# Four chained layers on one core: the second layer's first operands rounded inside the first layer's drain, and the last MLP map taken by quarters

## The chip, the core and the metric

The kernel runs on one core of one Trainium2 chip. A core has five engines that work side by side and meet only through semaphores: TensorE (PE in the profile, its weight loads PEld), VectorE (DVE), ScalarE (ACT), GpSimd (POOL) and SyncE (SP), which issues the DMAs here. The metric is the device time of the whole program in microseconds (us). The kernel before took 1287.68 us in the median of three runs (1285.73 to 1287.99).

## What is computed

Four layers follow one another on 16 sequences of 128 x 256 values (batch B = 16, D = 256). The change touches the end of layer 0 and the start of layer 1.

```python
# layer 0, its end: the MLP
ln_out = layernorm(x, ln3_s, ln3_b)
mlp_out = gelu(ln_out @ w1 + b1) @ w2 + b2        # 256 -> 1024 -> 256
x = x + mlp_out
# layer 1, its start: x is z1ss, the context is u1ss; columns 0:128 and 128:256 have their own weights
for i in range(2):
    h = einsum('od,bdl->bol', Wqkv[i], z1ss[:, :, s:e])
    h = h + einsum('od,bdl->bol', Winj[i], u1ss[:, :, s:e])
    chunks.append(h)
q, k, v = split(concatenate(chunks, axis=2), 3, axis=1)     # 16 heads of 64
# then per head: softmax((q + r_w_bias) . k * SCALE) . v, a map Wo, the residual, a norm
```

Layers 2 and 3 (a small attention and a second product of maps with a batch norm) end the program; nothing of them is changed but the address of one tensor.

## The kernel before

**Blocks.** `program` runs two blocks one after the other, `layer0` and `layers123`. Each gives every engine its own list of instructions. All engines meet at the end of a block, so no instruction of the second starts before the last of the first.

**Layer 0** takes the batch in eight pairs. It is a software pipeline of `BODIES` = 13 bodies. In a body several pairs are at different steps, and the order of an engine's work is written out by hand in its `body`: `pairs(step, offset)` does a step for the pair that stands at that offset, and leaves it out where there is none. The last bodies are the drain, with ever fewer pairs. In body 11 the last pair (the eighth) is at the transposes of its normalised values (T2) and the four hidden maps f0 to f3, while the pair before is at its two output maps y0 and y1, one per batch. In body 12 the last pair has its y0 and y1 and nothing else is left. The linear maps take turns in two PSUM banks, and a map may start when the one before it in its bank has been read out.

The hidden values `hid` are eight chunks of 128 features. They are made in four quarters of two chunks each: PE's map f (L529), two readings by ACT into `ring_h` and `ring_g` (L719), a polynomial and a product on DVE (L884, L889), tanh on ACT (L727), and the gate on DVE (L896). Each gate adds one to `h_gate`. PE's y0 waits for `h_gate.at(i, 3)`, the fourth quarter, and then takes all eight chunks, and y1 follows (L538). In PSUM the sum over the chunks is built up in place. DVE adds `x_mlp` and writes `xs` (L905). `x_mlp` is made by POOL (L447).

**Layer 1** takes the batch in eight pairs again. It multiplies in a faster float format (fp32r) and keeps the accuracy by splitting each operand into a rounded high part and the rest: `wzh`, `wih` are high parts of the weights for the input and for the context, `wzl`, `wil` the rests, `zuh`, `zul` the same of the two inputs (`xs` and `l1_ub`). A projection is high x high + high x rest + rest x high for both inputs and both column halves: 12 matmuls (L1722 for q and k, L1726 for v). ACT casts to the high parts (L1890, L1898, L1903). DVE subtracts to get the rests of the inputs (L1987, L1992) and of the `wz` weights (L2034), POOL those of the `wi` weights (L1676). A rest is written over the raw weight. The weights are rounded in twelve parts, `qk0`, `v0`, `qk1`, ..., of which the first `AT_ONCE` = 4 are made at the start of the block and the others one by one in the first eight steps of the first pair. PE starts with three projections, q0, k0 and v0b0. ACT rounds q0 and k0 again into `qh` and `kh`, DVE makes `ql` and `kl` (L1977, L1981) and copies v0b0 (L1972), and by that frees the bank; q0 and v0b0 share one. Then come the steps, 16 per pair: scores (L1740), row maxima (L1950), exponentials (L1861), the division (`norm`, POOL, L1664), the transposes (L1752), the product with v (L1768) and, in the gaps, the next projections. The last map's weights `wo` are loaded at the block's start (L1653), rounded on ACT (L1943) and their rest made on POOL (L1701), ahead of the first step.

In the second block SP first adds each event's starting credit (one instruction each, some 25), and only then issues its first DMA.

Of the kernel before, what the change touches and what calls it, by code (L numbers as in the profile page):

```python
# [87 lines left out]
def program(nc, x, ctx_in, ctxT, smask, cmask, cols_in, rows_in, wqkv_in, wao_in, wq_in, wkv_in, wco_in,  # L88
            w1_in, w2_in, wz_in, wi_in, wo_in, wqk2_in, wvpg_in, theta_in, ww_in, out, dbg=None, phases="ABC"):
    with ExitStack() as ctx:  # L90
        def sb(name, shape, c=ctx):
# [15 lines left out]
        raw_place = ExitStack()  # L107
        wz0_raw, wz1_raw, wi0_raw, wi1_raw = (raw_place.enter_context(nc.sbuf_tensor(n, [P, 3 * NQ], F32)) for n in (
            "wz0_raw", "wz1_raw", "wi0_raw", "wi1_raw"))
# [6 lines left out]
        if "A" in phases:  # L116
            layer0(nc, locals())
        raw_place.close()
        wzl0, wzl1, wil0, wil1 = (ctx.enter_context(nc.sbuf_tensor(n, [P, 3 * NQ], F32R)) for n in (
            "wzl0", "wzl1", "wil0", "wil1"))  # L120
# [12 lines left out]
def layer0(nc, v):  # L133
    (psum, xs, ident, mean_w, cols, half_neg, col) = (v[n] for n in (
        "psum", "xs", "ident", "mean_w", "cols", "half_neg", "col"))
    (l1_weights_in, wz0_raw, wz1_raw, wi0_raw, wi1_raw) = (v[n] for n in (
        "l1_weights_in", "wz0_raw", "wz1_raw", "wi0_raw", "wi1_raw"))
# [14 lines left out]
    with ExitStack() as ctx:  # L152
# [13 lines left out]
        rows = sb("rows", [P, ROWS["bvpg"]])  # L166
# [3 lines left out]
        wkv = sb("wkv", [P, 2, 2 * D])  # L170
        wco = sb("wco", [P, 2, D])
# [8 lines left out]
        cT = sb("cT", [P, 2, TOK])  # L180
# [77 lines left out]
        def start(bank):  # L258
# [24 lines left out]
            sem(f"weights_in_{n}") for n in ("cols", "rows", "qkv", "ao", "kv", "q", "co", "1", "2", "mask"))  # L283
        consts_made = sem("consts_made")
# [59 lines left out]

        block = ctx.enter_context(nc.Block())

        @block.sync
        def _(sp):
# [48 lines left out]
            for w, src, c in ((wz0_raw, "wz_in", 0), (wz1_raw, "wz_in", 1), (wi0_raw, "wi_in", 0),  # L397
                              (wi1_raw, "wi_in", 1)):
                sp.dma_start(w[:, :], v[src][c * P:(c + 1) * P, :]).then_inc(l1_weights_in, 16)
            for g in range(3, R0 + 2):  # L400
# [5 lines left out]
            sp.dma_start(v["ub"][:, :, :], v["ctx_in"].rearrange("b p d -> p b d")[:, 0:2, :])\  # L406
                .then_inc(v["first_u_in"], 16)
            sp.wait_ge(l1_weights_in, 64)
            sp.wait_ge(v["first_u_in"], 16)

        @block.gpsimd
        def _(pool):
# [47 lines left out]

            def body(j, g):
# [12 lines left out]
                units(add_mask, 7)  # L474

# [29 lines left out]
        def _(pe):  # L505
# [35 lines left out]

            def linear(i, g, name):
# [29 lines left out]
                elif name[0] == "f":  # L572
# [3 lines left out]
                    features_out(i, name, w1, m * 2 * P, lnT[2], g)  # L576
                else:
# [125 lines left out]
        def _(act):  # L703
# [57 lines left out]

            def body(j, g):
# [18 lines left out]
                pairs(read, -1, "k")  # L781
                pairs(read, -4, "T2")
# [51 lines left out]
        def _(dve):  # L834
# [134 lines left out]

            def body(j, g):  # L970
# [27 lines left out]
                units(invert, -4)  # L998

# [55 lines left out]
class Turns:  # L1055
# [31 lines left out]
    def reads(self, key):  # L1087
# [5 lines left out]
          (("x2", 2, 2, D), ("x2b", 2, 2, D), ("fin", 2, 2, D)))  # L1093


def third_stage(nc, v, ctx, late, joins):
# [7 lines left out]
    prob, pT, x2, x2b, fin = (late[n] for n in ("l2_prob", "l2_pT", "x2", "x2b", "fin"))  # L1104
# [17 lines left out]
    vpg = sb("vpg", [P, 2, 2, 2, D])  # L1122
# [369 lines left out]
def layers123(nc, v):  # L1492
    (sb_, psum, xs, ident, mean_w, half_neg, col) = (v[n] for n in (
        "sb", "psum", "xs", "ident", "mean_w", "half_neg", "col"))
    (wz0_raw, wz1_raw, wi0_raw, wi1_raw, wzl0, wzl1, wil0, wil1) = (v[n] for n in (
        "wz0_raw", "wz1_raw", "wi0_raw", "wi1_raw", "wzl0", "wzl1", "wil0", "wil1"))
# [8 lines left out]
    with ExitStack() as ctx:  # L1505
# [30 lines left out]
        wi = [[sb(f"wih{c}", [P, 3 * NQ], F32R) for c in range(2)], [wil0, wil1]]  # L1536
        wo = [sb("woh", [P, PAIRS, P], F32R), wol]
        zu = [sb(f"zu{p}", [P, 2, 2, NB, P], F32R) for p in ("h", "l")]
# [7 lines left out]
        ub, first_u_in = v["ub"], v["first_u_in"]  # L1546
# [15 lines left out]
        PARTS = ["qk0", "v0", "qk1", "qk2", "v1", "qk3", "qk4", "v2", "qk5", "qk6", "v3", "qk7"]  # L1562
        AT_ONCE = 4
# [593 lines left out]
```

## Time and profile before

| | before |
|---|---|
| median of 3 runs | 1287.68 us |
| profiled execution, its own time | 1287.96 us |
| its span, first to last instruction | 1286.2 us |
| granted TensorE clock, mean (share of full) | 0.985 |
| PE busy | 1210.8 us (94%) |
| DVE busy | 927.3 us (72%) |
| ACT busy | 825.9 us (64%) |
| POOL busy | 548.8 us (43%) |

The span runs from the first instruction to the last; the time of a run holds a little more around it. Busy time is the sum of an engine's instructions. Matmuls overlap one another and their ends are modelled, so PE's busy time says little of its rate. The last instruction of layer 0 ends at 469.87 us, layers 2 and 3 begin near 1200 us.

### The profile page before, as it was taken

The numbers are of one execution on the slowest core, as the hardware profiler recorded it, in microseconds if no ns is written. First come the engines' busy times: TensorE is split into PE (matmuls) and PEld (weight loads), VectorE is DVE, ScalarE is ACT, GpSimd is POOL, SyncE is SP. The second block draws the span as 40 slices with busy tenths as digits, with TensorE's granted clock in tenths as the row PEclk, the third lists the DMA queues.
The fourth block names the chain that finished last, engine by engine and source line by source line (L and its number), as shares of the span: only waits on it lengthen the run. The fifth ranks groups of instructions, "written<-read, shape, count | busy, mean of one in ns | idle before, by whom it ended". The sixth has DMA issues, their size and how long they took to land.

```text
span 1286.2 us, 29854 instructions
## 1 busy us (share of the span) xinstructions
PE 1210.8 (94%) x10914; PEld 995.1 (77%) x10914; DVE 927.3 (72%) x1835; ACT 825.9 (64%) x2523; POOL 548.8 (43%) x535
## 2 busy tenths in 40 slices
PE   4798999999999869999999999999999999999997
PEld 3677787788887658888888888888888888888675
DVE  4779989889887558776666676766766766666664
ACT  4588978978986548655555555565555555565542
POOL 3456656546644126433333333334333333333443
PEclk8899999999999979999999999999999999999999
DMA  3340000000000000000000000000000100000011
GB/s 105 99 197 19 14 22 9 12 12 17 6 22 1 1 25 2 2 10 1 2 10 2 1 10 2 8 3 2 10 2 2 55 1 2 1 2 2 18 42 41
DMA packets 18575, 25.39 MB, mean 20 GB/s; under 512 B 1424, under 2 KB 17040, under 8 KB 17936
## 3 DMA queue, kind: packets, MB, share of 16 engines
q1 hardware_dynamic: 18448, 23.69, 5.6%
q8 instruction: 81, 1.33, 0.4%
q14 instruction: 46, 0.38, 0.1%
HBM read 21.58 MB, written 2.10 MB: 18 GB/s over the span
## 4 chain that ended last, share of the span: by engine, by line
PE 49%; ACT 7%; DVE 5%; issue 2%; ACTq 0%
PE psum L1722 11%; PE psum L1768 8%; PE psum L1752 8%; PE psum L1740 7%; PE psum L1726 5%; ACT prob L1861 4%; PE psum L1777 3%; ACT pT L1870 1%; DVE l_neg_max L1950 1%; PE psum L1258 1%; PE psum L1322 1%; PE psum L1793 1%; ACT aTh L1876 1%; DVE aTl L1966 1%; PE psum L1272 1%
## 5 line engine op out<-in xcount | busy, mean ns | idle before, releaser
L1664 POOL TENSOR_TENSOR prob<-prob,l_z_inv 128x512 f32<-128x512 f32 x256 | 261.0, 1040 | 440.5 <-DVE l_z_inv L1956 440.5
L1861 ACT ACTIVATE prob<-psum,l_neg_max 128x256 f32<-128x256 f32 x512 | 235.6, 472 | 228.0 <-DVE l_neg_max L1950 227.9
L752 ACT ACTIVATE ring_e<-ring_e,neg_max 128x128 f32<-128x128 f32 x512 | 164.2, 406 | 15.1 <-DVE neg_max L921 15.0
L1950 DVE TENSOR_REDUCE l_neg_max<-psum 128x2 f32<-128x512 f32 x256 | 163.8, 681 | 10.8 <-PE psum L1740 10.8
L1752 PEld LDWEIGHTS psum<-ident,prob 128*128 128x128 f32 x1024 | 109.8, 141 | 49.0 <-issue 45.0
L1768 PE MATMUL psum<-pT,vs 128*64 128x256 f32 x1024 | 138.8, 391 | 3.7 <-DVE aTl L1966 3.5
L1752 PE MATMUL psum<-ident,prob 128*128 128x128 f32 x1024 | 139.9, 280 | 0.0
L459 POOL TENSOR_TENSOR ring_e<-ring_e,cross_add 128x512 f32<-128x512 f32 x64 | 85.7, 1356 | 91.4 <-DVE ring_e L916 91.4
L1961 DVE COPY pT<-psum 128x512 f32<-128x512 f32 x128 | 88.0, 688 | 45.5 <-PE psum L1752 45.3
L459 POOL TENSOR_TENSOR ring_e<-ring_e,self_add 128x512 f32<-128x512 f32 x64 | 85.9, 1356 | 64.0 <-DVE ring_e L916 63.3
L1966 DVE TENSOR_TENSOR aTl<-psum,aTh 128x256 fp32r<-128x256 f32 x128 | 54.3, 425 | 74.6 <-ACT aTh L1876 74.6
L760 ACT COPY ring_t<-psum 128x512 f32<-128x512 f32 x128 | 75.2, 588 | 47.6 <-PE psum L603 46.9
L1861 ACT ACTIVATION_READ_ACCUMULATOR prob<-psum,l_neg_max 128x1 f32 x512 | 104.0, 203 | 0.0
L1768 PEld LDWEIGHTS psum<-pT,vs 128*64 128x64 f32 x1024 | 63.6, 136 | 39.6 <-issue 7.3
L603 PE MATMUL psum<-ident,ring_e 128*128 128x128 f32 x512 | 82.2, 285 | 10.0 <-ACT ring_t L760 9.1
L1740 PE MATMUL psum<-kh,qh 64*128 64x256 f32 x512 | 85.8, 329 | 5.2 <-ACT prob L1861 5.2
L603 PEld LDWEIGHTS psum<-ident,ring_e 128*128 128x128 f32 x512 | 62.0, 145 | 34.6 <-issue 14.3
L921 DVE TENSOR_REDUCE neg_max<-ring_e 128x4 f32<-128x512 f32 x128 | 84.8, 673 | 2.3 <-POOL ring_e L459 2.3
L1722 PE MATMUL psum<-zuh,wzh 128*128 128x256 f32 x256 | 74.4, 291 | 4.7 <-POOL wil L1676 4.7
L1870 ACT COPY pT<-psum 128x512 f32<-128x512 f32 x128 | 76.3, 596 | 0.2 <-PE psum L1752 0.2
L1740 PE MATMUL psum<-kl,qh 64*128 64x256 f32 x512 | 72.9, 278 | 0.0
L1722 PE MATMUL psum<-zuh,wih 128*128 128x256 f32 x256 | 72.8, 284 | 0.0
(190 smaller groups left out, 3181.2 us busy)
## 6 DMA issues: line engine op xcount, KB each, us to landing
wz_raw<-wz_in SPq DMA_DIRECT2D x2, 1536.0 KB, 14.3
wi_raw<-wi_in SPq DMA_DIRECT2D x2, 1536.0 KB, 20.1
x_in<-x SPq DMA_DIRECT2D x8, 256.0 KB, 2.8
cT<-ctxT SPq DMA_DIRECT2D x8, 256.0 KB, 2.8
w<-w_in SPq DMA_DIRECT2D x2, 1024.0 KB, 8.5
l_ub<-ctx_in SPq DMA_DIRECT2D x8, 256.0 KB, 2.8
cg<-ctx_in SPq DMA_DIRECT2D x4, 512.0 KB, 4.2
out<-fin SPq DMA_DIRECT2D x8, 256.0 KB, 2.1
```

The source lines that it names most:

```text
L459: pool.tensor_tensor(e, e, add, ALU.add).then_inc(scores_add.sem, 1)
L603: last = nc.tensor.transpose(turn_bank[:, h * P:(h + 1) * P], ring_e[:, n % RE, h * P:(h + 1) * P], ident[:, :])
L752: last = nc.scalar.activation(e, e, ACT.Exp, bias=neg_max[:, n % RE, h:h + 1])
L1664: pool.tensor_tensor(e, e, z_inv[:, t % RE, h, :].unsqueeze(2).broadcast_to([P, 2, D]), ALU.mult)\
L1722: last = mm(o, w[wp][c][:, at:at + P], zu[xp][:, s, c, :, :].rearrange("p b l -> p (b l)"), **flags)
L1740: last = mm(score_bank[h][:, qt * D:(qt + 1) * D], q[qp][rows, pair % 2, qt, b, :], k[kp][rows, pair % 2, :, b, :], start=(qp, kp) == (0, ...
L1752: last = nc.tensor.transpose(turn_bank[h][:, kt * D + qt * P:kt * D + (qt + 1) * P], prob[:, t % RE, h, qt * D + kt * P:qt * D + (kt + 1) ...
L1768: last = mm(pv_bank[h * HD1:(h + 1) * HD1, :], vs[:, pair // 2 % 2, b, kt, at:at + HD1], pT[:, h, kt * D:(kt + 1) * D], start=kt == 0, sto ...
L1861: last = nc.scalar.activation(prob[:, t % RE, h, qt * D:(qt + 1) * D], score_bank[h][:, qt * D:(qt + 1) * D], ACT.Exp, bias=neg_max[:, t % ...
L1870: nc.scalar.copy(pT[:, 0, :], turn_bank[0]).then_inc(copied[0].sem, 1)
L1950: nc.vector.tensor_reduce(neg_max[:, t % RE, h, :], score_bank[h].rearrange("p (t c) -> p t c", t=2), AX.X, ALU.max, negate=True).then_inc ...
L1961: nc.vector.tensor_copy(pT[:, 1, :], turn_bank[1]).then_inc(copied[1].sem, 1)
```

## The change

Two things are changed.

The first is the last pair's output map. `last_outputs` takes it in eight groups of two chunks: batch 0 with quarters 0 and 1, batch 1 with quarters 0 and 1, then quarters 2 and 3 with the batches in turns. Each group waits for its own quarter.

The second is the rounding of what layer 1 needs for q0, k0 and v0b0. It moves from the start of the second block into body 11 of layer 0 (`ROUNDING`): ACT casts the first columns of q, k and v of the four raw weights into `first_hi`, and both inputs of the first pair into `zu[0]`; DVE makes the rests of the `wz` weights and of the inputs, POOL those of the `wi` weights. The new tensors lie over `wqkv`, `wao`, `wq`, `wkv` and `cT`, which nobody reads any more by then. The first context pair `l1_ub` is loaded right behind the raw weights instead of at the end of layer 0. In layer 1 the parts `qk0` and `v0` fall away, `AT_ONCE` is 2, and ACT and DVE handle q0 and k0 between the first part and the second. `vpg` of the third stage gets another address.

```diff
+        with ExitStack() as c:
+            zu = [c.enter_context(nc.sbuf_tensor(f"zu{p}", [P, 2, 2, 2, P], F32R)) for p in ("h", "l")]
+            first_hi = c.enter_context(nc.sbuf_tensor("first_hi", [P, 4, 4, P], F32R))
...
+        ROUNDING = BODIES - 2
+
+        def early(w):
+
+            return (w[:, 0:2 * NQ].rearrange("p (t c) -> p t c", t=2)[:, :, 0:P],
+                    w[:, 2 * NQ:2 * NQ + D].rearrange("p (t c) -> p t c", t=2))
+
+        def early_inputs(s):
+
+            return (ub[:, :, :] if s else xs[:, 0:NB, :]).rearrange("p b (c l) -> p c b l", c=2)
...
+            sp.dma_start(ub[:, :, :], v["ctx_in"].rearrange("b p d -> p b d")[:, 0:2, :]).then_inc(first_u_in, 16)
             for g in range(3, R0 + 2):
                 next_ctx(g - 2)
...
             sp.wait_ge(w_mask, 16)
-            sp.dma_start(v["ub"][:, :, :], v["ctx_in"].rearrange("b p d -> p b d")[:, 0:2, :])\
-                .then_inc(v["first_u_in"], 16)
-            sp.wait_ge(l1_weights_in, 64)
-            sp.wait_ge(v["first_u_in"], 16)
...
+            def early_rests():
+                for n in (2, 3):
+                    for k, (low, raw) in enumerate(zip(early(lows[n]), early(raws[n]))):
+                        pool.wait_ge(early_hi, 4 * k + n + 1)
+                        pool.tensor_tensor(low, raw, first_hi[:, n, 2 * k:2 * k + 2, :].bitcast(F32), ALU.subtract)
...
                 units(add_mask, 7)
+                if g == ROUNDING:
+                    early_rests()
...
+            def last_outputs(i, g):
+
+                for quarter, b in ((0, 0), (1, 0), (0, 1), (1, 1), (2, 0), (2, 1), (3, 0), (3, 1)):
+                    name = f"y{b}"
+                    ps = bank(name, i) if quarter == 0 else lin(name)
+                    pe.wait_ge(*h_gate.at(i, quarter))
+                    for c in (2 * quarter, 2 * quarter + 1):
+                        last = nc.tensor.matmul(ps[:, 0:D], hid[:, c, b * P:(b + 1) * P], w2[:, c, 0:D],
+                                                start=c == 0, stop=c == F0 // P - 1)
+                    if quarter == 3:
+                        filled(name, last, g)
...
+                elif g == R0 - 1:
+                    if name == "y0":
+                        last_outputs(i, g)
...
+            def early_rounding():
+                act.wait_ge(l1_weights_in, 64)
+                act.wait_ge(first_u_in, 16)
+                for k in range(2):
+                    for n, raw in enumerate(raws):
+                        nc.scalar.copy(first_hi[:, n, 2 * k:2 * k + 2, :], early(raw)[k]).then_inc(early_hi, 1)
+                    nc.scalar.copy(zu[0][:, k, :, :, :], early_inputs(k)).then_inc(early_zu_hi, 1)
...
                 pairs(read, -1, "k")
+                if g == ROUNDING:
+                    early_rounding()
                 pairs(read, -4, "T2")
...
+            def early_rests():
+                for k in range(2):
+                    for n in range(2):
+                        dve.wait_ge(early_hi, 4 * k + n + 1)
+                        nc.vector.tensor_tensor(early(lows[n])[k], early(raws[n])[k],
+                                                first_hi[:, n, 2 * k:2 * k + 2, :].bitcast(F32), ALU.subtract)
+                    dve.wait_ge(early_zu_hi, k + 1)
+                    nc.vector.tensor_tensor(zu[1][:, k, :, :, :], early_inputs(k), zu[0][:, k, :, :, :].bitcast(F32),
+                                            ALU.subtract)
...
                 units(maxima, 4)
                 units(invert, -4)
+                if g == ROUNDING:
+                    early_rests()
...
-        PARTS = ["qk0", "v0", "qk1", "qk2", "v1", "qk3", "qk4", "v2", "qk5", "qk6", "v3", "qk7"]
-        AT_ONCE = 4
+
+        PARTS = ["qk1", "qk2", "v1", "qk3", "qk4", "v2", "qk5", "qk6", "v3", "qk7"]
+        AT_ONCE = 2
...
-                if isinstance(i, int) and i == 0:
+                if i == 0 and rounded(name):
                     pe.wait_ge(z_lo_made, rounded(name))
                     pe.wait_ge(i_lo_made, rounded(name))
...
-            round_z(0)
             round_part(0)
-            round_u(0)
+            for name in AHEAD[:2]:
+                round_work(0, name)
             for n in range(1, AT_ONCE):
                 round_part(n)
-            for name in AHEAD[:2]:
-                round_work(0, name)
...
-            rest_z(0)
             rest_part(0)
-            rest_u(0)
+            for name in AHEAD[:2]:
+                rest_work(0, name)
             for n in range(1, AT_ONCE):
                 rest_part(n)
-            for name in AHEAD:
+            for name in AHEAD[2:]:
                 rest_work(0, name)
```

How the instructions stand at two places. In these rows `w,hid` is a matmul of the output map, `[waits ...]` names the semaphores that an instruction waits for, and a second layer's product reads `zuh` or `zul` and a weight.

TensorE, the end of layer 0 and the first matmuls of layer 1, before:

```order
L529 MATMUL psum<-lnT,w 128x256 [waits linear0_read_out]
L529 MATMUL psum<-lnT,w 128x256 x3
L538 MATMUL psum<-w,hid 128x256 [waits linear1_read_out,h_gate]
L538 MATMUL psum<-w,hid 128x256 x7
L538 MATMUL psum<-w,hid 128x256 [waits linear0_read_out]
L538 MATMUL psum<-w,hid 128x256 x7
L152 UNCONDITIONAL_BRANCH
L1704 UNCONDITIONAL_BRANCH [waits barrier_Pool_Activation_PE_DVE_SP_release]
L1722 MATMUL psum<-zuh,wzh 128x256 [waits l1_work_bank0_read_out,l1_zu_lo,i_weights_lo_made,z_weights_lo_made]
```

The same place after the change:

```order
L576 MATMUL psum<-w,hid 128x256 [waits h_gate,linear1_read_out]
L576 MATMUL psum<-w,hid 128x256
L576 MATMUL psum<-w,hid 128x256 [waits h_gate]
L576 MATMUL psum<-w,hid 128x256
L576 MATMUL psum<-w,hid 128x256 [waits h_gate,linear0_read_out]
...
L576 MATMUL psum<-w,hid 128x256 [waits h_gate]
L576 MATMUL psum<-w,hid 128x256
L160 UNCONDITIONAL_BRANCH
L1779 UNCONDITIONAL_BRANCH [waits barrier_Pool_Activation_PE_DVE_SP_release]
L1797 MATMUL psum<-zuh,first_hi 128x256 [waits l1_zu_lo,l1_work_bank0_read_out]
```

The sixteen matmuls are the same; they stand in eight groups with a wait each, and the first of layer 1 no longer waits for rests of weights.

VectorE, from the previous pair's first output to the last pair's first polynomial, before, and the start of layer 1:

```order
L905 SCALAR_TENSOR_TENSOR xs<-psum,x_mlp 128x256 [waits residual2_biased,linear1_full]
L884 TENSOR_SCALAR ring_g<-ring_g 128x512 [waits linear1_read_out]
...
L1946 UNCONDITIONAL_BRANCH [waits barrier_Pool_Activation_PE_DVE_SP_release]
L1987 TENSOR_TENSOR zul<-xs,zuh 128x512 [waits l1_zu_hi]
```

and after:

```order
L957 SCALAR_TENSOR_TENSOR xs<-psum,x_mlp 128x256 [waits residual2_biased,linear1_full]
L1026 TENSOR_TENSOR wzl<-wz_raw,first_hi 128x2x128 [waits early_hi] x2
L1029 TENSOR_TENSOR zul<-xs,zuh 128x512 [waits early_zu_hi]
L1026 TENSOR_TENSOR wzl<-wz_raw,first_hi 128x256 [waits early_hi] x2
L1029 TENSOR_TENSOR zul<-l_ub,zuh 128x512 [waits early_zu_hi]
...
L2014 UNCONDITIONAL_BRANCH [waits barrier_Pool_Activation_PE_DVE_SP_release]
L2102 TENSOR_TENSOR wzl<-wz_raw,wzh 128x2x128 [waits weights_hi_made] x2
L2045 SCALAR_TENSOR_TENSOR ql<-psum,cols,qh 128x512 [waits l1_work_hi]
L2049 SCALAR_TENSOR_TENSOR kl<-psum,kh 128x512 [waits l1_work_hi]
L2102 TENSOR_TENSOR wzl<-wz_raw,wzh 128x2x128 [waits weights_hi_made] x2
L2040 COPY vs<-psum 128x512 [waits l1_work_bank0_full]
```

Six subtractions now stand in the drain, and at the start of layer 1 two rests instead of eight lie ahead of `ql`.

## Rows read from the trace of the kernel before

**Rows 1.** PE by stretch: us, busy (matmuls), granted clock, DMA share, GB/s

```profile
458.00:460.00 2.00, 0.26 (x1) 0.50 0.00 0
...
476.00:478.00 2.00, 2.00 (x12) 0.50 0.03 12
```

**Rows 2.** All engines by stretch, layer 1: PE, PEld, DVE, ACT, POOL busy, clock

```profile
480.00:560.00 80.00, 79.14 (x692) 66.89 (x691) 61.41 (x132) 56.30 (x186) 43.67 (x46) 1.00 0.01 2
```

**Rows 3.** PE in time: start, us, what, count, [idle before, releaser]

```profile
437.66 3.69 PE L538 MATMUL psum<-w,hid 128*128 128x256 f32 x16 [1.82 <-DVE x L876]
441.19 0.60 PE L520 MATMUL psum<-ident,ln 128*128 128x128 f32 x4
...
453.51 1.99 PE L529 MATMUL psum<-lnT,w 128*128 128x256 f32 x8 [1.66 <-ACT ring_g L719]
459.74 9.61 PE L538 MATMUL psum<-w,hid 128*128 128x256 f32 x32 [4.23 <-DVE hid L896]
474.01 0.55 PE L1722 MATMUL psum<-zuh,wzh 128*128 128x256 f32 x1 [4.66 <-POOL wil L1676]
...
479.47 0.36 PE L1726 MATMUL psum<-wzh,zuh 128*128 128x256 f32 x1 [0.44 <-DVE ql L1977]
...
481.06 0.39 PE L1740 MATMUL psum<-kh,qh 64*128 64x256 f32 x2
```

**Rows 4.** DVE in time, from the last normalisation to the first `ql`

```profile
439.73 0.74 DVE L850 TENSOR_SCALAR ln<-x,mean_var,rstd 128x256 f32<-128x256 f32 x2 [1.09 <-POOL rstd L439]
...
446.59 0.43 DVE L884 TENSOR_SCALAR ring_g<-ring_g 128x512 f32<-128x512 f32 x1 [4.72 <-ACT ring_g L719]
448.51 0.42 DVE L905 SCALAR_TENSOR_TENSOR xs<-psum,x_mlp 128x256 f32<-128x256 f32 x1 [1.50 <-PE psum L538]
...
454.01 0.69 DVE L896 SCALAR_TENSOR_TENSOR hid<-ring_g,ring_h 128x512 f32<-128x512 f32 x1 [1.09 <-ACT ring_g L727]
...
458.21 1.47 DVE L896 SCALAR_TENSOR_TENSOR hid<-ring_g,ring_h 128x512 f32<-128x512 f32 x2
...
469.45 0.42 DVE L905 SCALAR_TENSOR_TENSOR xs<-psum,x_mlp 128x256 f32<-128x256 f32 x1 [3.04 <-PE psum L538]
...
473.25 5.31 DVE L2034 TENSOR_TENSOR wzl<-wz_raw,wzh 128x256 fp32r<-128x256 f32 x6
478.48 0.74 DVE L1977 SCALAR_TENSOR_TENSOR ql<-psum,cols,qh 128x512 fp32r<-128x512 f32 x1
```

**Rows 5.** ACT in time, the drain and the new block's start

```profile
441.88 1.02 ACT L708 ACTIVATE lnT<-psum,cols 128x256 f32<-128x256 f32 x2 [5.70 <-PE psum L520]
...
456.27 0.84 ACT L719 ACTIVATE ring_g<-psum,cols 128x256 f32<-128x256 f32 x2
...
470.18 0.62 ACT L1890 CAST zuh<-xs 128x512 fp32r<-128x512 f32 x1 [11.22 <-PEq L152]
470.70 0.71 ACT L1903 CAST wzh<-wz_raw 128x256 fp32r<-128x256 f32 x2
```

**Rows 6.** POOL in time, the drain and the new block's start

```profile
449.08 1.58 POOL L447 TENSOR_TENSOR x_mlp<-x,rows 128x512 f32<-128x512 f32 x1 [9.38 <-DVE xs L905]
471.79 7.36 POOL L1676 TENSOR_TENSOR wil<-wi_raw,wih 128x256 fp32r<-128x256 f32 x8 [21.13 <-ACT wih L1903]
480.68 2.39 POOL L1701 TENSOR_TENSOR wol<-wol_raw,woh 128x1024 fp32r<-128x1024 f32 x1 [1.53 <-ACT woh L1943]
484.10 2.04 POOL L1664 TENSOR_TENSOR prob<-prob,l_z_inv 128x512 f32<-128x512 f32 x2 [1.03 <-DVE l_z_inv L1956]
```

**Rows 7.** The normalisation's line, 300 to 445 us: ns min/median/max, first and last start

```profile
L850 DVE TENSOR_SCALAR ln<-x,mean_var,rstd x12: 400/537/1365, 318.8 to 440.1; 128x256 f32<-128x256 f32 x12
```

**Rows 8.** SP's first DMA of layer 1, and its landing (KB, us)

```profile
471.65 0.37 SPq L1653 DMA_DIRECT2D wol_raw<-wo_in  x1
...
wol_raw<-wo_in SPq DMA_DIRECT2D x1, 512.0 KB, 4.0
```

More of the change, by code:

```diff
@@ L104, in program @@
         first_u_in = ctx.enter_context(nc.semaphore("first_u_in"))
-        raw_place = ExitStack()
-        wz0_raw, wz1_raw, wi0_raw, wi1_raw = (raw_place.enter_context(nc.sbuf_tensor(n, [P, 3 * NQ], F32)) for n in (
-            "wz0_raw", "wz1_raw", "wi0_raw", "wi1_raw"))
+        with ExitStack() as c:
+            wz0_raw, wz1_raw, wi0_raw, wi1_raw = (sb(n, [P, 3 * NQ], c) for n in (
+                "wz0_raw", "wz1_raw", "wi0_raw", "wi1_raw"))
+        wzl0, wzl1, wil0, wil1 = (ctx.enter_context(nc.sbuf_tensor(n, [P, 3 * NQ], F32R)) for n in (
+            "wzl0", "wzl1", "wil0", "wil1"))
+        with ExitStack() as c:
+            zu = [c.enter_context(nc.sbuf_tensor(f"zu{p}", [P, 2, 2, 2, P], F32R)) for p in ("h", "l")]
+            first_hi = c.enter_context(nc.sbuf_tensor("first_hi", [P, 4, 4, P], F32R))
         l1_weights_in = ctx.enter_context(nc.semaphore("l1_weights_in"))
@@ L117, in program @@
             layer0(nc, locals())
-        raw_place.close()
-        wzl0, wzl1, wil0, wil1 = (ctx.enter_context(nc.sbuf_tensor(n, [P, 3 * NQ], F32R)) for n in (
-            "wzl0", "wzl1", "wil0", "wil1"))
+        sb("rounded_early", [P, 32 * P])
         if "B" in phases:
@@ L135, in layer0 @@
         "psum", "xs", "ident", "mean_w", "cols", "half_neg", "col"))
-    (l1_weights_in, wz0_raw, wz1_raw, wi0_raw, wi1_raw) = (v[n] for n in (
-        "l1_weights_in", "wz0_raw", "wz1_raw", "wi0_raw", "wi1_raw"))
+    (l1_weights_in, first_u_in, ub, zu, first_hi) = (v[n] for n in (
+        "l1_weights_in", "first_u_in", "ub", "zu", "first_hi"))
+    raws, lows = ([v[n + e] for n in ("wz", "wi") for e in ends] for ends in (("0_raw", "1_raw"), ("l0", "l1")))
     NB = 2
@@ L170, in layer0 @@
         wkv = sb("wkv", [P, 2, 2 * D])
+        cT = sb("cT", [P, 2, TOK])
+        rows = sb("rows", [P, ROWS["bvpg"]])
         wco = sb("wco", [P, 2, D])
@@ L1103, in third_stage @@
     HALVES = B // 2
-    prob, pT, x2, x2b, fin = (late[n] for n in ("l2_prob", "l2_pT", "x2", "x2b", "fin"))
+    prob, pT, x2, x2b, fin, vpg = (late[n] for n in ("l2_prob", "l2_pT", "x2", "x2b", "fin", "vpg"))
     def sb(name, shape):
@@ L1535, in layers123 @@
         wz = [[high(f"wzh{c}", LATE_3[c]) for c in range(2)], [wzl0, wzl1]]
-        wi = [[sb(f"wih{c}", [P, 3 * NQ], F32R) for c in range(2)], [wil0, wil1]]
+        wi = [[high(f"wih{c}", LATE_3[2 + c]) for c in range(2)], [wil0, wil1]]
         wo = [sb("woh", [P, PAIRS, P], F32R), wol]
-        zu = [sb(f"zu{p}", [P, 2, 2, NB, P], F32R) for p in ("h", "l")]
         q = [sb(f"q{p}", [P, 2, 2, NB, P], F32R) for p in ("h", "l")]
@@ L1716, in project @@
                     o = ps[:, c * D:(c + 1) * D]
-                    for s, w in enumerate((wz, wi)):
+                    for s in range(2):
                         for wp, xp in ((0, 0), (0, 1), (1, 0)):
                             flags = {"start": (s, wp, xp) == (0, 0, 0), "stop": (s, wp, xp) == (1, 1, 0)}
+                            w = columns(s, wp, c, name)
                             if name[0] in "qk":
-                                at = "qk".index(name[0]) * NQ + int(name[1]) * P
-                                last = mm(o, w[wp][c][:, at:at + P],
-                                          zu[xp][:, s, c, :, :].rearrange("p b l -> p (b l)"), **flags)
-                            else:
-                                at = 2 * NQ + int(name[1]) * D
-                                last = mm(o, zu[xp][:, s, c, int(name[3]), :], w[wp][c][:, at:at + D], **flags)
+                                last = mm(o, w, zu[xp][:, s, c, :, :].rearrange("p b l -> p (b l)"), **flags)
+                            else:
+                                last = mm(o, zu[xp][:, s, c, int(name[3]), :], w, **flags)
                 last.then_inc(work.fills(name), 1)
```

36 lines of the change are left out of this document (20 added, 16 removed).

## Prediction, made before the changed kernel was run

> **What bounds the kernel now.** I read the stretches first. From 480 us on TensorE (PE) is busy 79.14 of 80 us at the full granted clock [rows 2]: the second layer is bound by PE, so what comes earlier at its start comes earlier at the end. Before that stands the drain of the first layer, and there PE waits. Its last product of the MLP (32 matmuls, two maps of 16) begins at 459.74, 4.23 us after PE ran out of work, because all eight chunks of `hid` are asked for before the first is used [rows 3]. The clock is at half (1.2 GHz) when it begins [rows 1]. VectorE (DVE) reads the last map out until 469.87 [rows 4]. ScalarE (ACT) then opens the next block at 470.18 [rows 5], PE works from 474.01, at half clock again [rows 1], and the first scores start at 481.06 [rows 3]. So two stretches hold the change: 455.5 to 469.9 and 469.9 to 481.1.
>
> What ends the waits in the second? PE's first projection is named as waiting for a rest made by POOL (GpSimd) [rows 3]. But the tail is DVE's: six rests take 5.31 from 473.25, and only at 478.48 comes `ql` [rows 4], which frees the bank for the value map at 479.47 [rows 3]. The scores stand behind that map in PE's order.
>
> **The last MLP map in quarters.** The same 32 matmuls, now in eight groups of four. f3's matmuls end at 455.5 (453.51 + 1.99), and the groups can follow at once. Sixteen such matmuls take 3.69 at full clock [rows 3], so 32 take 7.4 or a little less, since the 3.69 holds the pipelined end of the last. I take 7.2, a group 0.9. The waits: quarters 0 and 1 of `hid` exist by 454.7 (454.01 + 0.69) [rows 4]. Map y1 needs ACT to have read f3, at 457.11 (456.27 + 0.84) [rows 5]; PE comes there at 457.3. Quarter 2 is made at 458.95 (half of 1.47 after 458.21), quarter 3 at 459.68 [rows 4]; PE comes at 459.1 and 460.9. No group waits. PE ends at 462.7 instead of 469.35 (459.74 + 9.61), the last output 6.65 earlier, at 463.2. **Gain 6.65**, of which the clock is 9.61 − 7.2 = 2.4.
>
> **Rounding moved into the drain.** ACT does eight casts (0.71 a pair) and two of 128x512 at 0.62 [rows 5]: 4 x 0.71 + 2 x 0.62 = 4.1 at most, placed before it reads T2. There it stands idle for 5.70 until 441.88 [rows 5]: covered, 1.6 to spare. DVE does four rests and two of 128x512. Beside POOL the six at the join took 5.31 / 6 = 0.89 each [rows 4], so 4 x 0.89 + 2 x 0.89 x 2 = 7.1 at most (a double width counted double); half of that where POOL is quiet. It starts behind the output of the pair before, at about 441.9. The next step began at 446.59 after 4.72 of idle, and what follows it waits for PE's y1 until 448.51 [rows 4]. The likely 4 is covered, the 7.1 would stick out by 0.5 (441.9 + 7.1 against 448.51). POOL does four rests at 7.36 / 8 = 0.92, so 3.7, in the 9.38 of idle before 449.08 [rows 6]: covered. Without these covers the three would cost 4.1, up to 7.1, and 3.7.
>
> One piece is not free. POOL's rests start right behind `rstd`, which is what DVE's last normalisation waits for (439.73, 0.74 for its two parts [rows 4]). A part of it takes 400 ns at its shortest and 1365 at its longest [rows 7]. If both parts are lengthened it ends up to 1.9 later than 440.47. PE's transposes behind it could start only at 441.19 anyway, since PE was on the previous pair's y0 until then [rows 3]. Neither end is nearer, so I take half of the lengthening: the end comes at 441.45, **loss 0.3** (0 to 1.2). From there on the drain is a chain, so it reaches the end. The page SBUF — State Buffer of the Trainium skill (section Who interferes with whom) says that a VectorE instruction with two inputs in SBUF, or a `tensor_scalar` in a two-port mode, and a GpSimd instruction that reads SBUF shut each other out for the whole instruction. By that rule the normalisation would wait for whole rests of POOL, and the loss would be nearer to the upper end, 0.9 more than I take; the spread of rows 7 agrees with it.
>
> **The moved DMA.** `l1_ub` is loaded behind the four weight loads, near 60 us, in SP's queue ahead of the next context load. No wait of PE in the rows is for a load, so zero.
>
> **The block start.** Let S be the new block's start on ACT, 0.31 after the last output. Before, PE began at S + 3.83 and the scores at S + 10.88. Now PE waits only for SP's first increments: SP issues its first DMA at S + 1.47 [rows 8], after some 25 of them, and the needed ones are the first eight. PE starts at S + 0.5. q0 and k0, 24 matmuls, took 5.0 before (474.01 to 479.03, the 0.44 of wait before 479.47 taken off), mostly at half clock; the value map's 12 took 1.59 at the full one [rows 3], so they take 2 x 1.5. q0 is full at S + 2.1; ACT rounds it until 2.8; `ql` takes 0.74 [rows 4], until 3.6; the value map runs from 3.85 and the scores start at S + 5.4. **Gain 5.5.** PE's pause between the blocks is 1.3 (462.7 + 0.3 to S + 0.5). In the trace half clock stood behind waits of 4.23 and 4.66 [rows 1, 3].
>
> **What is late next.** `wo`'s load leaves at S + 1.5 and takes 4.0 [rows 8], so ACT can round it only from S + 5.5 to 6.5. POOL's rest of it takes 2.39 [rows 6] and ends at S + 9.0. Behind it in POOL's order stands the first normalisation, which before began 3.04 after the scores (484.10) [rows 6], now S + 8.4. So it is 0.6 late, and PE's turns with it. **Loss 0.5** (0 to 1.5, if ACT's first exponentials are late too). The later parts keep their places in the steps.
>
> **Sum.** 6.65 + 5.5 − 0.3 − 0.5 = 11.35. The profiled execution took 1287.96 (span 1286.2), so 1276.6; the median shown is 0.28 below it: 1276.3.
>
> **Rivals.**
> 1. Half clock stays, by the pause at the block start or by eight waits in the groups. The clock was low behind both long waits of PE here [rows 1]; against it, the pause now is a third of those. q0 and k0 then cost 2.0 more, the groups 2.4: 1278.3 to 1280.7.
> 2. PE isn't ready at S + 0.5. No row shows when PE could start in the new block, since its first instruction waited until S + 3.83; ACT's was ready after 0.31. At the worst the start loses those 3.3 and the clock its 2.0: 1281.6; midway 1279. The page Runtime: NRT & Kernel Launch of the Trainium skill (Instruction fetch mechanics) says that a taken branch out of the sequencer's window stalls for a fetch. By that rule the time is this rival's; no row here shows such a stall on PE.
> 3. Slower than before: the rounding in the drain comes in series instead of side by side, through the port that rows 7 hint at and ACT's handing on. Its place is 436.2 to 449, its price 4.1 + 7.1 + 3.7 = 14.9; less 11.35 that is 3.5 slower, 1291.5. It decides once more than 11.35 is uncovered. The idle times of 5.70, 4.72 and 9.38 lie in parallel and speak against it.
> 4. The quarters bring less: a group that waits holds all behind it, since PE takes them in order. If the waits for ACT and DVE cost 2 in sum, 1278.3.
> 5. More than forecast: no loss at either place, 12.2 or a little over: 1275.
>
> **Numbers.** Forecast, 1274.8 to 1278.2: 73%. Rival 1: 9%. Rival 2: 9%. Rival 4: 4%. Below 1274.8: 3%. Rival 3: 2%. The range that leaves under 2 in 10 out is 1274.5 to 1279.8. A measurement of this kernel can tell about 0.2% (2.6 us). Faster by more than that 0.97, within it 0.02, slower 0.01.
>
> **What would show it.** PE without a pause over 0.3 from f3's matmuls to the last of the groups, at granted clock 1.00; the last output near 463.5; the two parts of the last normalisation at 1.3 to 1.8 in sum; PE's first projection 0.5 after ACT's first cast of the new block; the first scores 5.4 behind that cast; POOL's rest of `wo` directly ahead of the first normalisation. It would be wrong if the clock reads 0.5 in either stretch, or if PE in the second layer shows waits that it didn't have.

## The result, and the profile after

The changed kernel takes 1275.04 us in the median of six runs (1274.21 to 1275.77), the kernel before 1287.08 beside it (1283.56 to 1288.12). The ratio is 0.9917, with a 95% interval of 0.9906 to 0.9928, so 10.7 us faster, give or take 1.4. The two medians alone are 12.0 apart, at the edge of that interval; single runs of the kernel before spread over 4.6 us. The prediction said 1276.3 and 11.35 us. The profiled execution took 1274.89, its span 1273.2.

| | before | after |
|---|---|---|
| span of the profiled execution | 1286.2 | 1273.2 |
| granted TensorE clock, mean | 0.985 | 0.991 |
| PE busy | 1210.8 (94%) | 1204.5 (95%) |
| DVE, ACT, POOL busy | 927.3, 825.9, 548.8 | 927.0, 825.9, 547.2 |

The work is the same; PE's busy time is 6 less, and less of it runs at half clock: the last map's 32 matmuls are 2.3 shorter, for example. Line numbers have shifted (L538 is L565 or L576, L1722 is L1797, L1740 is L1813, L850 is L902). PE from the seventh pair's y0 to the second step, as [rows 3] (start, us, what, count, idle before it and what ended it):

```profile
434.99 3.69 PE L565 MATMUL psum<-w,hid 128*128 128x256 f32 x16 [1.82 <-DVE x L928]
438.67 0.66 PE L547 MATMUL psum<-ident,ln 128*128 128x128 f32 x4
...
451.05 1.99 PE L556 MATMUL psum<-lnT,w 128*128 128x256 f32 x8 [1.66 <-ACT ring_g L761]
452.88 7.33 PE L576 MATMUL psum<-w,hid 128*128 128x256 f32 x32
461.60 0.36 PE L1797 MATMUL psum<-zuh,first_hi 128*128 128x256 f32 x1 [1.39 <-SPq L1722]
...
466.46 0.39 PE L1813 MATMUL psum<-kh,qh 64*128 64x256 f32 x2
...
470.70 0.39 PE L1813 MATMUL psum<-kh,qh 64*128 64x256 f32 x2 [0.20 <-ACT prob L1934]
...
472.34 0.66 PE L1825 MATMUL psum<-ident,prob 128*128 128x128 f32 x4 [0.66 <-POOL prob L1739]
473.34 0.66 PE L1825 MATMUL psum<-ident,prob 128*128 128x128 f32 x4 [0.34 <-POOL prob L1739]
...
484.15 0.36 PE L1799 MATMUL psum<-wzh,zuh 128*128 128x256 f32 x1
```

The 32 matmuls of the last map stand behind f3 without a wait and take 7.33. PE's first projection waits 1.39 and is released by SP's increments. The first scores come 4.86 behind it. The granted clock is 1.00 in both places (453 to 460.2 and 461.6 to 466.4 us). Three short waits in the second step are new, 1.20 in all.

ACT, DVE and POOL in the drain and at the block start, as [rows 4 to 6]:

```profile
433.42 0.70 ACT L809 CAST first_hi<-wz_raw 128x256 fp32r<-128x256 f32 x2
...
439.42 1.02 ACT L750 ACTIVATE lnT<-psum,cols 128x256 f32<-128x256 f32 x2 [2.43 <-PE psum L547]
...
461.05 0.71 ACT L1973 CAST wzh<-wz_raw 128x256 fp32r<-128x256 f32 x2 [4.55 <-PEq L160]
...
467.77 1.05 ACT L2011 CAST woh<-wol_raw 128x1024 fp32r<-128x1024 f32 x1 [1.23 <-DMA wol_raw<-wo_in]
468.73 0.47 ACT L1934 ACTIVATE prob<-psum,l_neg_max 128x256 f32<-128x256 f32 x1
```

```profile
437.06 1.55 DVE L902 TENSOR_SCALAR ln<-x,mean_var,rstd 128x256 f32<-128x256 f32 x2 [1.09 <-POOL rstd L458]
...
444.12 0.43 DVE L936 TENSOR_SCALAR ring_g<-ring_g 128x512 f32<-128x512 f32 x1 [1.86 <-ACT ring_g L761]
```

```profile
437.00 3.11 POOL L484 TENSOR_TENSOR wil<-wi_raw,first_hi 128x256 fp32r<-128x256 f32 x4
446.61 1.59 POOL L466 TENSOR_TENSOR x_mlp<-x,rows 128x512 f32<-128x512 f32 x1 [6.50 <-DVE xs L957]
...
468.90 2.39 POOL L1776 TENSOR_TENSOR wol<-wol_raw,woh 128x1024 fp32r<-128x1024 f32 x1 [0.88 <-ACT woh L2011]
471.25 2.04 POOL L1739 TENSOR_TENSOR prob<-prob,l_z_inv 128x512 f32<-128x512 f32 x2
```

The early rounding is hidden: ACT still idles 2.43 ahead of `lnT`, DVE 1.86 behind its rests, POOL 6.50. Behind the block start `wo` stands in the way: ACT waits 1.23 for its load, and POOL goes from its rest straight into the first normalisation (its idle time there is gone).

**Where the 13.0 of the two traces is.** I cut both at four points: M, PE's start on the seventh pair's y0; S, ACT's first cast of the new block; T, the first scores; U, the first value-map matmul behind the fourth scores, where the first pair's steps run evenly again. U in the kernel before is this row:

```profile
497.19 0.36 PE L1726 MATMUL psum<-wzh,zuh 128*128 128x256 f32 x1
```

The lengths between the points:

| | before | after | shorter by |
|---|---|---|---|
| start to M | 437.66 | 434.99 | 2.67 |
| M to S (drain) | 32.52 | 26.06 | 6.46 |
| S to T (block start) | 10.88 | 5.41 | 5.47 |
| T to U (first steps) | 16.13 | 17.69 | -1.56 |
| U to the end | 789.01 | 789.05 | -0.04 |

The change itself is worth 10.33 here. What was gained ahead of U arrives whole at the end. From M to U alone it is 10.37.

### The profile page after: what moved, and what is told of

Same layout as the page of the kernel before. It is cut to its first block, busy times and chain, and to the rows that moved or that the text cites. A ratio compares the mean times of both kernels' runs of the same rounds, so it can differ in the third digit from the quotient of the medians.

```text
span 1273.2 us, 29851 instructions
## 1 busy us (share of the span) xinstructions
PE 1204.5 (95%) x10914; PEld 989.7 (78%) x10914; DVE 927.0 (73%) x1835; ACT 825.9 (65%) x2523; POOL 547.2 (43%) x535
## 4 chain that ended last, share of the span: by engine, by line
PE 51%; ACT 6%; DVE 3%; issue 2%; DMA 0%; POOL 0%; ACTq 0%; SPq 0%
PE psum L1797 12%; PE psum L1841 9%; PE psum L1825 9%; PE psum L1813 7%; PE psum L1799 5%; ACT prob L1934 3%; PE psum L1850 3%; ACT pT L1943 1%; PE psum L1322 1%; PE psum L1386 1%; DVE l_neg_max L2018 1%; DVE aTl L2034 1%; PE psum L1866 1%; PE psum L1336 1%; ACT aTh L1949 1%
## 5 line engine op out<-in xcount | busy, mean ns | idle before, releaser
L2018 DVE TENSOR_REDUCE l_neg_max<-psum 128x2 f32<-128x512 f32 x256 | 163.8, 681 | 10.7 <-PE psum L1813 10.6
L1813 PE MATMUL psum<-kh,qh 64*128 64x256 f32 x512 | 85.8, 329 | 5.4 <-ACT prob L1934 5.4
L1813 PE MATMUL psum<-kl,qh 64*128 64x256 f32 x512 | 72.8, 278 | 0.0
L1813 PE MATMUL psum<-kh,ql 64*128 64x256 f32 x512 | 72.5, 276 | 0.0
L1797 PE MATMUL psum<-zuh,wzl 128*128 128x256 f32 x256 | 72.2, 282 | 0.0
```

Of the source, the lines that this page charges most:

```text
L1797: last = mm(o, w, zu[xp][:, s, c, :, :].rearrange("p b l -> p (b l)"), **flags)
L1813: last = mm(score_bank[h][:, qt * D:(qt + 1) * D], q[qp][rows, pair % 2, qt, b, :], k[kp][rows, pair % 2, :, b, :], start=(qp, kp) == (0, ...
L2018: nc.vector.tensor_reduce(neg_max[:, t % RE, h, :], score_bank[h].rearrange("p (t c) -> p t c", t=2), AX.X, ALU.max, negate=True).then_inc ...
```

## The experiments

The theory has three terms and one exclusion: the quarters 6.65, the block start 5.5, a loss at the first steps that is `wo`'s, and ahead of M only what single executions differ by. The rivals are named in the expectations. M, S, T and U are the points of the table above, and "ratio" is the time against the kernel before.

**The changed kernel again.** No edit.

> The changed kernel itself. In its trace the stretch from PE's start on the seventh pair's y0 to the second step's value map is 38.8 us against 49.1 before, so the change is worth 10.4; the other 2.7 of the two traces' difference lies ahead of it, in the clock of the first 65 us. Theory A (the 2.7 is the wobble of single executions, not the change's): the ratio to before, over five rounds, stands at 10.4 of 1287, 0.9919. Rival B (the new addresses in layer 0 or the earlier load of l1_ub save it): 13 of 1287, 0.990, in every round.

1275.42 in the median (five runs), ratio 0.9915 [0.9902, 0.9929]. Its profiled run had M at 437.84, where the same program had it at 434.99 before. PE's granted clock tells which it was. PE from 60 to 70 us in before, after and after_again (us, busy, clock, DMA share, GB/s):

```profile
60.00:70.00 10.00, 9.73 (x92) 0.73 1.04 408
```

```profile
60.00:70.00 10.00, 9.11 (x118) 1.00 1.04 413
```

```profile
60.00:70.00 10.00, 9.70 (x92) 0.74 1.04 402
```

Over the twelve profiled executions of this study M lies between 434.99 and 438.37 with no order in the edits: quarters_only, which has the addresses and the loads of before, 437.58; warm_wait, which has them too, 435.71. It goes with the clock of that one stretch: where the granted clock from 60 to 70 us is 0.72 to 0.75 (five executions), M is at 437.17 or later, and where it is 0.80 or more (seven), at 436.07 or earlier. So the 2.67 is not the change's, and rival B's ratio of 0.990 lies outside the interval. M to S, S to T and T to U were 26.06, 5.41 and 17.28, so M to U was 10.78 shorter than before.

**The quarters alone.**

```diff
 (on the kernel before)
+            def last_outputs(i, g):
...
+                elif g == R0 - 1:
+                    if name == "y0":
+                        last_outputs(i, g)
```

> The kernel before with last_outputs alone; addresses, loads and the rounding at the start of layer 1 as before. The prediction's own term: 6.65 faster, y's 32 matmuls in 7.2 to 7.4 at full clock and no wait. PE then idles about 4.7 before its first projection, as before, so the start block costs what it did (10.9 from ACT's first cast to the first scores). If the terms of the two parts add up, this and rounding_only together give 10.4. If B holds this kernel's layer 0 is as long as before's up to the seventh pair's y0 (437.7), and rounding_only's is 2.7 shorter.

1278.89, ratio 0.9945 [0.9932, 0.9959]: 7.1 faster. In the trace:

```profile
455.27 7.33 PE L549 MATMUL psum<-w,hid 128*128 128x256 f32 x32
467.26 0.36 PE L1737 MATMUL psum<-zuh,wzh 128*128 128x256 f32 x1 [4.66 <-POOL wil L1691]
...
472.74 0.35 PE L1741 MATMUL psum<-wzh,zuh 128*128 128x256 f32 x1 [0.88 <-DVE ql L1992]
474.33 0.39 PE L1755 MATMUL psum<-kh,qh 64*128 64x256 f32 x2
```

The map takes 7.33 at granted clock 1.00. M to S is 25.85, 6.67 shorter: the term to 0.02. S to T stays 10.90 and T to U 16.13. The value map waits for `ql` longer (0.88 against 0.44): q0 and k0 were quicker here, and DVE's six rests bound the block start all the same.

**The rounding alone.**

```diff
 (on the changed kernel)
-                elif g == R0 - 1:
-                    if name == "y0":
-                        last_outputs(i, g)
```

> The changed kernel with y0 and y1 taken as before (all chunks after the last gate, one batch after the other). Expected: y 9.6 after a wait of 4.2, at half clock for its first 5; start of layer 1 as in the changed kernel: PE's first projection 0.5 after ACT's first cast, scores 5.4 behind it, second step late by 1.5. So 5.5 - 0.2 - 1.5 = 3.8 faster than before. A rival says that the parts lean on each other through the clock: the y maps end at full clock here too, so none is expected.

1282.02, ratio 0.9971 [0.9961, 0.9981]: 3.7 faster, with 3.8 expected. The trace says more, 5.34 from M to U, for two reasons. y took 8.86 here and not 9.61, after the same wait of 4.23: the half clock ended earlier in this execution (clock 0.50 from 460 to 462 us, 0.99 from 462 on; before, 0.50 until 464.7). And T to U is 16.79, a loss of 0.66 and not the 1.5 that was expected, as `wo`'s load took 4.1 and ACT did not wait for it. S to T is 5.42.

```profile
457.61 8.86 PE L565 MATMUL psum<-w,hid 128*128 128x256 f32 x32 [4.23 <-DVE hid L945]
467.86 0.35 PE L1794 MATMUL psum<-zuh,first_hi 128*128 128x256 f32 x1 [1.39 <-SPq L1719]
```

By the runs 7.1 and 3.7 make 10.8, and both together give 10.7. By the traces 6.65 and 5.34 make 11.99; less the 0.75 of y and the 0.90 and 0.49 by which the later steps lost more in the two traces of the changed kernel, that is 10.34 and 10.75, against 10.37 and 10.78. The parts add up.

**Wait and clock apart.**

```diff
 (on the kernel before)
+                    if name == "y0" and g == R0 - 1:
+                        for _ in range(9):
+                            nc.tensor.matmul(score_bank[0][:, 0:TOK], w1[:, 0, 0:P], lnT[2][:, 0, :], start=True, stop=True)
                     if name == "y0":
                         pe.wait_ge(*h_gate.at(i, 3))
```

> The kernel before, with nine matmuls without use (128x256, some 0.43 each at full clock) put into PE's wait of 4.23 ahead of the last y0. Their result is read by nobody; all that the kernel before computes is there. It takes the two parts of the quarter term apart: the wait stays, only the granted clock can change. Theory: with PE busy in the wait the clock stays at 1.00 and y's 32 matmuls take 7.2 instead of 9.6: 2.4 faster than before. Then of the 6.65 of the quarters 2.4 is the clock and 4.2 the wait. Rival: the clock falls all the same (the low share of work before counts), and the time is before's.

Ratio 0.9988 [0.9977, 0.9999], 1.5 faster (0.1 to 3.0). In the trace the map takes 7.17 at granted clock 1.00, where [rows 3] had 9.61 and the clock was 0.50 until 464.7:

```profile
457.81 7.17 PE L538 MATMUL psum<-w,hid 128*128 128x256 f32 x32 [0.35 <-DVE hid L899]
```

M to S is 30.10, 2.42 shorter than before. So the quarters' 6.67 is 4.2 of wait and 2.4 of clock, and matmuls without use buy back the second alone. The interval of the runs holds the 2.4 but can't size it; the trace does.

**The batches in turns.**

```diff
-                for quarter, b in ((0, 0), (1, 0), (0, 1), (1, 1), (2, 0), (2, 1), (3, 0), (3, 1)):
+                for quarter, b in ((0, 0), (1, 0), (2, 0), (3, 0), (0, 1), (1, 1), (2, 1), (3, 1)):
```

> The changed kernel with the eight groups in another order: batch 0's four quarters, then batch 1's. Quarters 2 and 3 of batch 0 then meet their gates (458.95 and 459.68 in the trace of before, when PE would come there at 457.3 and 459.9): a wait of 1.65 in the first and none in the second, so y ends 1.6 later than in the changed kernel: 1.6 slower than it, if the turns are what fills the wait. Rival: PE would not have been in time anyway and the order is free: 0.

1277.42, ratio 0.9933 [0.9919, 0.9947]; the changed kernel's two intervals (0.9906 to 0.9928 and 0.9902 to 0.9929) overlap this one, so the runs alone leave it open. The trace doesn't:

```profile
453.82 1.89 PE L576 MATMUL psum<-w,hid 128*128 128x256 f32 x8
457.43 5.45 PE L576 MATMUL psum<-w,hid 128*128 128x256 f32 x24 [1.72 <-DVE hid L948]
```

PE waits 1.72 for the third gate, M to S is 27.79, 1.73 longer than with turns. The turns are a quarter of the gain of the quarters.

**POOL's early rests later.**

```diff
                 units(add_mask, 7)
-                if g == ROUNDING:
-                    early_rests()
...
                 pairs(add_bias, -4, 2, x_mlp, x_2, "b2", "y1")
+                if g == ROUNDING:
+                    early_rests()
```

> The changed kernel, but POOL makes its four early rests behind x_mlp instead of right behind rstd. Then nothing of POOL runs beside DVE's last normalisation and the early rests of DVE. Theory: the normalisation's two parts take 0.74 again instead of 1.55 and DVE's early rests 4 x 0.37 and 2 x 0.65; the transposes behind start 0.15 to 0.2 earlier, which the time can't show (under 0.1%). Rival: the 1.55 has another cause (ACT's casts beside it, the clock of the memory) and stays.

```profile
440.45 0.74 DVE L902 TENSOR_SCALAR ln<-x,mean_var,rstd 128x256 f32<-128x256 f32 x2 [1.09 <-POOL rstd L458]
...
442.50 0.75 DVE L1026 TENSOR_TENSOR wzl<-wz_raw,first_hi 128x256 fp32r<-128x256 f32 x2
```

On DVE the normalisation takes 0.74 again instead of 1.55, and DVE's first two rests 0.75, where in the changed kernel they take 1.28. So POOL's work beside them was the cause. M to S is 25.86, 0.20 shorter. The time (1275.3, ratio 0.9917 [0.9901, 0.9932]) can't show it. The Trainium skill, SBUF — State Buffer, section Who interferes with whom, says that such instructions and GpSimd's shut each other out. It agrees with the direction, and the size here is 0.81 for two instructions, about one rest of POOL (3.11 / 4 = 0.78).

**The second pair's input behind `wo`.**

```diff
+            sp.wait_ge(wo_in, 16)
             for i in range(1, R1):
                 sp.wait_ge(*zu_lo.at(i - 1, 1))
                 load_u(i)
```

> The changed kernel, but SP waits for wo's load before it issues the second pair's l1_ub. In the changed kernel's trace wo's load left at 462.51 and ACT could round it only at 467.77, 5.26 later, where it took 4.0 before; l1_ub's load went 0.43 behind it. Theory: the two loads share the DMA engines, and alone wo's lands 1.1 to 1.3 earlier; ACT's first exponentials then start 1.1 earlier, until the maxima stop them (468.12): 0.6 earlier, and POOL's rest of wo ends 1.1 earlier, so the first normalisation 1.1 earlier and the time 1.0 to 1.1 shorter. Rival: wo's load is slow for another reason (its own descriptors, cold queue), and nothing moves.

Ratio 0.9918 [0.9905, 0.9932], T to U 17.13. That is 0.15 and 0.56 less than in the two traces of the changed kernel, not the 1.0 of the theory: this theory falls. The load of `wo` took this long (KB, us to landing) in the changed kernel, and with nothing behind it:

```profile
wol_raw<-wo_in SPq DMA_DIRECT2D x1, 512.0 KB, 5.2
```

```profile
wol_raw<-wo_in SPq DMA_DIRECT2D x1, 512.0 KB, 4.7
```

The same load took 4.8 in after_again, 4.6 in no_turns, 5.1 in pool_later, 5.6 in wo_halves and 4.1 in rounding_only, all with the input's load issued 0.4 behind it, and 4.0, 4.0 and 3.8 in before, quarters_only and warm_wait, where it is issued 1.7 behind. The second load explains little of it.

The DMA traces point at something else, a packet of instructions (the profile's queue `q8 instruction`, one packet of 0.02 MB). In five executions it starts within 0.2 us of `wo`'s first packets:

| | packet, us | load of `wo`, us | difference |
|---|---|---|---|
| after | 1.8 | 5.2 | 3.4 |
| after_again | 1.4 | 4.8 | 3.4 |
| no_turns | 1.1 | 4.6 | 3.5 |
| pool_later | 1.6 | 5.1 | 3.5 |
| ub_behind_wo | 1.3 | 4.7 | 3.4 |

The load's length follows the packet's to 0.1 in these five, with or without the input's load behind it. In rounding_only the packet comes some 0.8 earlier (load 4.1), in wo_halves after the load's first packets (load 5.6), and in before, quarters_only and warm_wait there is none during the load. No run moved the packet, so that it lengthens the load is likely and not shown, and 3.4 is less than the 3.8 to 4.0 that the load took without one.

**`wo` in halves, behind the first two steps.**

```diff
-            act.wait_ge(wo_in, 16)
-            nc.scalar.copy(wo_hi, wo_in_place).then_inc(wo_hi_made, 1)
             rounds(act, body, tail)
...
+                    if first and t < 2:
+                        act.wait_ge(wo_in, 16)
+                        at = slice(t * 4 * P, (t + 1) * 4 * P)
+                        nc.scalar.copy(wo_hi[:, at], wo_in_place[:, at]).then_inc(wo_hi_made, 1)
 (and POOL's rest likewise, behind the same steps; PE's wait asks for both halves)
```

> The changed kernel, but wo is rounded in two halves behind the first and the second step's exponentials on ACT, and its rest is made by POOL behind the normalisations of those steps, 1.2 each. Needed is it only at the fifth step. Theory: the 1.56 that the changed kernel loses between the first scores and the second step's value map (7.29 against 5.73 before) all stands behind wo; with wo out of the way the first normalisation starts 3.0 after the scores again and the time is 1.5 shorter than the changed kernel's (ratio to before 0.9908). Rival: POOL or ACT are just too full in the first steps, and the halves cost the same in the next ones: no change of the sum, with waits for POOL's prob in the second and third step.

1274.94, ratio 0.9911 [0.9897, 0.9925]. The first normalisation does start 3.03 behind the scores and the second step has no wait. But the third and the fourth have one each:

```profile
479.25 0.66 PE L1828 MATMUL psum<-ident,prob 128*128 128x128 f32 x4 [0.32 <-POOL prob L1739]
...
484.24 0.65 PE L1828 MATMUL psum<-ident,prob 128*128 128x128 f32 x4 [0.27 <-POOL prob L1739]
```

T to U is 17.11. That is 0.17 and 0.58 less than in the two traces of the changed kernel. Most of the loss has moved, as the rival said: POOL has little room in the steps in which it also makes parts.

**`wo` loaded early, with and without another place.** POOL's room is ahead of the scores. wo_loaded_early has the first hunk alone, wo_first both. Not shown: `wo_early` becomes the raw place of `wo`, and its load at the block's start goes.

```diff
+            wo_early = sb("wo_early", [P, H1 // 2, P], c)
...
+            sp.wait_ge(*of_pair(scores_done, R0 - 1, R0 - 1, 0, U - 1))
+            sp.dma_start(v["wo_early"][:, :, :], v["wo_in_dram"].rearrange("(h r) o -> r h o", r=P)).then_inc(v["wo_in"], 16)
```

```diff
             round_part(0)
+            act.wait_ge(wo_in, 16)
+            nc.scalar.copy(wo_hi, wo_in_place).then_inc(wo_hi_made, 1)
             for name in AHEAD[:2]:
                 round_work(0, name)
...
-            for n in range(AT_ONCE):
-                rest_part(n)
+            rest_part(0)
             pool.wait_ge(wo_hi_made, 1)
             pool.tensor_tensor(wo_lo, wo_in_place, wo_hi.bitcast(F32), ALU.subtract).then_inc(wo_lo_made, 1)
+            for n in range(1, AT_ONCE):
+                rest_part(n)
```

> The changed kernel, but wo is loaded at the end of layer 0's loads (its raw place is where the first q operand lay), ACT rounds it right behind the first weight part, where it waited 0.93 us for q0, and POOL makes its rest between the two parts, where it stood idle for 2.75. Theory: the loss behind the block start (17.69 and 17.28 us from the first scores to the first value map of the fourth group in the two traces of the changed kernel, 16.13 before) is wo's place in the two queues and its load together; then this stretch reads 16.1 to 16.2 and the time is 1.2 to 1.5 shorter than the changed kernel's. Rival: the first steps are full on POOL and ACT whatever stands ahead of them, as the halves of wo made POOL late in the third and fourth step: 17.0 or more, and nothing gained.

> The same early load of wo, but its rounding and its rest stay where the changed kernel has them. It parts the load from the place: ACT then rounds wo without the wait of 0.8 to 1.2 for the load, so the first exponentials start when the maxima are there and POOL's rest ends that much earlier. If the load is the larger part, the stretch from the first scores reads 16.2 to 16.6. If the place is (2.39 of POOL ahead of the first normalisation), it reads 16.8 or more.

wo_first: 1273.58, ratio 0.9903 [0.9886, 0.9920]. wo_loaded_early: 1272.87, ratio 0.9906 [0.9888, 0.9923]. By the runs neither can be told from the other or from the changed kernel. T to U is 16.12 and 16.79. In wo_first's trace POOL makes the rest between its two parts and has idle time ahead of the first normalisation again:

```profile
464.32 1.44 POOL L1756 TENSOR_TENSOR wil<-wi_raw,wih 128x256 fp32r<-128x256 f32 x2 [13.94 <-ACT wih L1979]
465.71 2.40 POOL L1780 TENSOR_TENSOR wol<-wo_early,woh 128x1024 fp32r<-128x1024 f32 x1
468.51 1.70 POOL L1756 TENSOR_TENSOR wil<-wi_raw,wih 128x256 fp32r<-128x256 f32 x2 [0.39 <-ACT wih L1979]
471.68 2.04 POOL L1744 TENSOR_TENSOR prob<-prob,l_z_inv 128x512 f32<-128x512 f32 x2 [1.47 <-DVE l_z_inv L2030]
```

So the loss is `wo`'s alone: 0.67 for its place (16.79 to 16.12), 0.5 to 0.9 for its load (17.28 and 17.69 to 16.79). The expectation had asked which is the larger; the two are of one size, and the load's share differs from execution to execution. rounding_only, where the load took 4.1, reads 16.79 too. With both away the stretch reads what it read before, and M to U is 47.60 against 59.53 before: 11.9 of gain. That makes wo_first the best version by its trace. The runs don't show it: its median is below the changed kernel's two, but 0.71 above wo_loaded_early's.

## Why the prediction was right

- **What bounds the kernel** held: from U to the end both traces agree within 0.04.
- **The quarters**, 6.65: 6.67 alone. 7.33 for the map where I took 7.2, and no group waited. Its split, 2.4 of clock, is shown by warm_wait (2.42).
- **Rounding in the drain, hidden**: shown by the idle times left on all three engines. ACT took 3.6 where I had up to 4.1, POOL 3.11 for 3.7, DVE 3.2 for the likely 4.
- **The normalisation**, loss 0.3: its lengthening was 0.81 (I took 0.95), the loss 0.20 by pool_later. By the rule of the Trainium skill (SBUF — State Buffer, Who interferes with whom) I had up to 0.9 more; that didn't come.
- **The block start**, 5.5: 5.47. PE began 0.55 behind ACT's first cast, released by SP's increments as worked out, at clock 1.00.
- **What is late next**, loss 0.5 (0 to 1.5): 1.56 and 1.15 in two traces, the first just outside the term's own range. This is the term that was mis-sized. I named the right queue and the right instruction, but took the load's 4.0 from one row as its price, and it took 4.6 to 5.6 in the six executions that have both parts of the change and load `wo` here. Where it took 4.1 (rounding_only) the loss was 0.66, near to what I had. And my middle value left the exponentials out: they start 2.27 behind the scores in after (1.84 in after_again) instead of 1.74. The prediction named as a sign that it is wrong that PE shows waits in the second layer that it didn't have. PE does, three with 1.20 in all, and they are this term's.
- The **sum** was 11.35. The stretches from M to U give 10.37 and 10.78, the runs 10.7 in the ratio. That 1275.04 still lies so near to the forecast 1276.3 is in part luck, as two errors cancel. The gain was some 0.6 to 1.0 smaller than forecast, and the time that it was taken from, 1287.96 less 0.28, was high: the kernel before had medians of 1286.32, 1286.67 and 1286.00 in the three later sets.
- **Rivals 1 and 2** (half clock, PE not ready) didn't come: the clock was 1.00 in both stretches. By the Trainium skill, Runtime: NRT & Kernel Launch, section Instruction fetch mechanics, there would have been a stall for a fetch behind the branch. No trace here shows one on PE, whose wait ends with SP's increments 0.55 behind ACT's first cast. **Rival 3** (slower) had nothing for it, as each engine kept idle time. **Rival 4** would have been the case without the turns: no_turns shows 1.73 of the 2.0 that I gave it.

## What to carry to other kernels

At a seam between two stages, ask for the operand that the first instruction needs, not for all that it will need: a wait on the last of several pieces costs the wait and, behind a wait of 4.23 as here, TensorE's clock (4.2 and 2.4 us; behind the waits of 1.39 and 1.72 the matmuls ran at full rate). Take two independent sums in turns, so that one covers the other's gate. Work moved out of a serial start brings everything behind it forward too: list what then stands next in each queue (here a load issued at the seam and one long instruction on GpSimd ahead of the first step) and give it a place in the idle time that is left ahead of the seam's end.

## What the runs showed that I had not expected

- The same program's first 435 us differ by up to 2.85 us from execution to execution (M at 434.99 and 437.84) with the granted clock of a single stretch (1.00 or 0.74 from 60 to 70 us). Two traces compared by their spans alone would have given the change 2.7 too much. Cut at common points, stretches of different kernels agreed within 0.03 (M to S: 26.05 to 26.06 in six executions of five kernels).
- The half clock behind one and the same wait of 4.23 lasted differently: y took 9.61 in before and 8.86 in rounding_only.
- A load of 512 KB at the same place of the program took between 3.8 and 5.6 us. In five executions its length follows that of a packet of instructions beside it (1.1 to 1.8), which no run has tested.
- Where an instruction stands counts for more than how it is cut: moving one instruction of 2.39 us on POOL, with ACT's cast ahead of it, into a gap of 2.75 us took 0.67 off the whole kernel's trace, while its two halves in busy steps (wo_halves) mostly moved the waits.
